# Second batch's kept parts on GpSimd's queue, other PSUM banks for scores and first values, other buffers for its keys, early fetches one by one

## What is computed

```python
x = L0_attn_x                                  # (2, 2048, 2048) float32, two batches
xn = (x - mean(x)) / sqrt(var(x) + 1e-5)       # over the last axis
q, k, v = split(xn @ Wqkv + bqkv, 3)           # 512 features each
attn = softmax(q @ k.T / sqrt(512)) @ v        # within a batch
gate = one_hot_softmax(top_k((xn @ Wq_w.T) @ keys.T, 16))   # 64 experts
z = (xn @ A_w.T) * gate                        # 64 experts x rank 8 = 512 features
out = x + attn @ Wo + bo + (z @ B_w.T) * 2.0
```

## Time and profile before

| | |
|---|---|
| median of 3 runs | 2750.1 us |
| the profiled execution | 2748.78 us, span 2746.8 us |
| granted clock of TensorE, mean over the span | 0.992 |
| TensorE | 97% busy, 11728 matmuls |
| VectorE, ScalarE, GpSimd | 68%, 36%, 18% busy |
| DMA | 648.29 MB, 236 GB/s on the mean |

### The profile page before, as it was taken

How to read it: one execution, slowest core, us unless ns; L and a number is a source line. 1 busy time by engine, 2 the same in 40 slices (tenths; PEclk the granted TensorE clock), 3 DMA queues, 4 the chain that set the end, 5 groups by cost and what they waited for, 6 DMA issues and landing times.

```text
span 2746.8 us, 32502 instructions
## 1 busy us (share of the span) xinstructions
PE 2655.9 (97%) x11728; PEld 2173.1 (79%) x11728; DVE 1856.9 (68%) x2311; ACT 976.5 (36%) x1289; POOL 494.5 (18%) x414
## 2 busy tenths in 40 slices
PE   6997999999999999999999999999998999999998
PEld 4776878878878888887887888887886888888787
DVE  6965876467755677676847476485773846658687
ACT  3562325622365224433334432224332233322311
POOL 1010000000000001111103332324213241232540
PEclk9999999999999999999999999999999999999999
DMA  8699666454564557766787758668676685866876
GB/s 308 203 342 290 230 207 200 147 167 153 170 207 148 175 182 239 236 211 237 265 301 254 265 193 291 230 241 322 232 273 261 220 312 196 292 229 231 299 260 221
DMA packets 256770, 648.29 MB, mean 236 GB/s; under 512 B 26720, under 2 KB 51424, under 8 KB 252384
## 3 DMA queue, kind: packets, MB, share of 16 engines
q1 hardware_dynamic: 205136, 487.80, 51.3%
q0 software_dynamic: 25616, 94.38, 9.5%
q10 hardware_dynamic: 25856, 63.99, 6.7%
HBM read 499.27 MB, written 146.83 MB: 235 GB/s over the span
## 4 chain that ended last, share of the span: by engine, by line
PE 84%; DMA 6%; DVE 5%; issue 2%; ACT 2%; SPq 0%; ACTq 0%; DVEq 0%
PE psum L803 36%; PE psum L1922 15%; PE psum L1924 15%; PE psum L1923 15%; DMA w_raw<-t_scratch 2%; PE psum L738 2%; DMA r_lo<-split_scratch 1%; DMA stat_scratch<-mv 1%; DVE w_lo L864 1%; ACT w_hi L524 1%; DMA w_raw<-W_blocks 1%; ACT rows L594 1%; PE psum L2008 0%; DVE s_lo L869 0%; DVE xb L951 0%
## 5 line engine op out<-in xcount | busy, mean ns | idle before, releaser
L864 DVE TENSOR_TENSOR w_lo<-w_raw,w_hi 128x1024 fp32r<-128x1024 f32 x224 | 274.0, 1223 | 386.4 <-ACT w_hi L524 386.3
L524 ACT ACTIVATE w_hi<-w_raw 128x1024 fp32r<-128x1024 f32 x224 | 237.5, 1060 | 735.0 <-PE psum L803 611.4
L803 PE MATMUL psum<-w_hi,s_hi 128*128 128x512 f32 x896 | 351.8, 393 | 22.4 <-DVE w_lo L864 21.3
L803 PE MATMUL psum<-s_hi,w_hi 128*128 128x512 f32 x896 | 352.3, 393 | 11.2 <-DVE s_lo L869 6.7
L803 PE MATMUL psum<-s_lo,w_hi 128*128 128x512 f32 x896 | 350.5, 391 | 0.0
L803 PE MATMUL psum<-w_lo,s_hi 128*128 128x512 f32 x896 | 350.3, 391 | 0.0
L803 PE MATMUL psum<-s_hi,w_lo 128*128 128x512 f32 x896 | 350.2, 391 | 0.0
L803 PE MATMUL psum<-w_hi,s_lo 128*128 128x512 f32 x896 | 350.2, 391 | 0.0
L803 PEld LDWEIGHTS psum<-w_hi,s_hi 128*128 128x128 f32 x896 | 169.1, 189 | 64.0 <-DVE w_lo L864 23.6
L2117 POOL TENSOR_TENSOR run_sum<-run_sum,prob 128x512 f32<-128x512 f32 x98 | 158.9, 1622 | 318.7 <-ACT prob L1761 311.7
L1922 PE MATMUL psum<-q_hi,r_hi 128*128 128x512 f32 x512 | 200.4, 391 | 11.9 <-issue 10.5
(11 more groups left out here) (197 smaller groups left out, 4945.9 us busy)
## 6 DMA issues: line engine op xcount, KB each, us to landing
r_hi<-split_scratch SPq DMA_DIRECT2D x208, 512.0 KB, 3.4
r_lo<-split_scratch SPq DMA_DIRECT2D x208, 512.0 KB, 4.5
w_raw<-t_scratch SPq DMA_DIRECT2D x128, 512.0 KB, 4.3
w_raw<-W_blocks SPq DMA_DIRECT2D x96, 512.0 KB, 3.9
split_scratch<-rows POOLq DMA_DIRECT2D x56, 512.0 KB, 4.2
part_out<-x POOLq DMA_DIRECT2D x28, 1024.0 KB, 12.5
out<-part_out SPq DMA_DIRECT2D x28, 1024.0 KB, 8.1
rows<-x ACTq DMA_DIRECT2D x26, 1024.0 KB, 5.1
```

Source lines behind the costliest of these rows:

```text
L524: nc.scalar.activation(w_hi[:, s % RAW], w_raw[:, s % RAW], ACT.Copy).then_inc(s_whi, 1)
L803: mm = pe.matmul(psum[:, bank, :], stationary, moving, start=(k == 0 and n == 0 and not chained), stop=(k == HK - 1 and n == 2), skip_grou ...
L864: nc.vector.tensor_tensor(w_lo[:, s % RAW], w_raw[:, s % RAW], w_hi[:, s % RAW].bitcast(F32), ALU.subtract).then_inc(s_wlo, 1)
```

## The change

- **Stores**: for t = 4, GpSimd issues the stores of kept parts (`keep` in its program), between the loads of x in S4 and between the sums in V4; they count on semaphores of their own (`b_late`). SyncE keeps only the first batch's. GpSimd's `scores(4)` loads two quarters of x (C22, C12), stores S4's items 0 to 3, loads C21 and C11, stores items 4 to 7, and then adds the bias.
- **Key buffers**: the raw tiles of S4 lie in eight places: items 0 to 3 in the quarters C11 and C21 of `part`, items 4 to 7 in `q_raw` and `p1_part`.
- **Banks**: scores of tiles 0 to 6 use banks 5, 2, 3, 4, 6, 0, 1. V0 uses banks 3, 4, 5, 6 and V1 banks 0, 1, 7, 6; the others stay with `BANK_B`.
- **V0**: the broadcast of group 1's maxima comes behind item 2 in place of item 1, and ScalarE takes it one item later.
- **Early fetches**: `ahead.sync` is called five times, at (5, 1), (5, 3), (5, 5), (5, 7) and (6, 1): first the queries, then one key item each.

```diff
@@ -133,6 +133,7 @@
 CHAINED = (1, 4, 6)
 SPLIT_TILES = 32
+AHEAD_AT = [(5, 1), (5, 3), (5, 5), (5, 7), (6, 1)]
@@ -490,8 +491,8 @@
                             store_kq(g, C22, b)
                             store_kq(g, C12, b)
-                    if not more and (idx, s) == (5, 1):
-                        ahead.sync(sp)
+                    if not more and (idx, s) in AHEAD_AT:
+                        ahead.sync(sp, AHEAD_AT.index((idx, s)))
                     if not more and idx == NI - 1 and s > PART:
@@ -1370,8 +1371,8 @@
         return (BANK_A, BANK_B)[(q + (w == NQ - 1)) % 2]
-    V_BANK = BANK_B
-    S_BANK = [(2 + k) % 7 for k in range(KEYT)]
+    V_BANKS = {0: [3, 4, 5, 6], 1: [0, 1, 7, 6]}
+    S_BANK = [(5, 2, 3, 4, 6, 0, 1)[k % 7] for k in range(KEYT)]
     S_LAST = [max(k for k in range(KEYT) if S_BANK[k] == b) if b < 7 else None for b in range(8)]
@@ -1401,8 +1402,14 @@
         return sum(1 if is_split(m) else 2 for m in range(n % RING, n + 1, RING))
-    def kept(n):
-        return sum(is_split(m) for m in range(n % RING, n, RING))
+    def slot_kept(engine, n):
+
+        before = [m for m in range(n % RING, n, RING) if is_split(m)]
+        late = [m for m in before if ITEMS[m][1] == BATCH]
+        if late:
+            engine.wait_ge(b_late[n % RING], 32 * len(late))
+        elif before:
+            engine.wait_ge(b_keep[n % RING], 32 * len(before))
@@ -1497,7 +1505,8 @@
         kind, t, i = ITEMS[n]
         if kind == "S" and t == BATCH:
-            return (q_raw, p1_part)[i % RING // 2][:, i % 2 * 2:i % 2 * 2 + 2, :]
+            tiles = (part[:, C11 * QT:(C11 + 1) * QT, :], part[:, C21 * QT:(C21 + 1) * QT, :], q_raw, p1_part)[i // 2]
+            return tiles[:, i % 2 * 2:i % 2 * 2 + 2, :]
         if t == 0:
@@ -1523,6 +1532,9 @@
         return attn[:, (w // 2 * 2 + row - 1) % 3, rows, :] if col == 1 else zT[:, row - 1, rows, :]
+    def bias_order(w):
+        return (C22, C12, C21, C11) if w == BATCH - 2 else (C22, C21, C12, C11)
+
     def out_quarter(w, c):
@@ -1548,6 +1560,9 @@
         return 2 * DT * ((t + 1) // 2)
+
+    def v_bank(t):
+        return V_BANKS.get(t, BANK_B)
@@ -1578,7 +1593,7 @@
         def keep_before(n):
-            while KEPT["next"] < len(SPLITS) and SPLITS[KEPT["next"]] < n:
+            while KEPT["next"] < 2 * LEN["S"] and SPLITS[KEPT["next"]] < n:
                 keep(SPLITS[KEPT["next"]])
@@ -1598,11 +1613,12 @@
                 if n >= RING and not is_split(n - RING):
                     sp.wait_ge(b_used, n - RING + 1)
-                if i < RING and t == BATCH and kind == "S":
-                    if i < 2:
-                        sp.wait_ge(b_qlo, 2 * (t + 1))
+                if t == BATCH and kind == "S":
+                    if i < 4:
+                        sp.wait_ge(b_st[(C11, C21)[i // 2]], 16 * 2)
                     else:
-                        sp.wait_ge(b_zt, z_done(t - 1))
+                        sp.wait_ge(b_lo, order - RING + 1)
+                        sp.wait_ge(b_qlo, 2 * (t + 1)) if i < 6 else sp.wait_ge(b_zt, z_done(t - 1))
                 elif i < RING and t == BATCH:
@@ -1683,19 +1699,18 @@
                     sp.dma_start(b_out[:], bo.rearrange("(a d) -> a d", a=1).to_broadcast([P, C])
                                  ).then_inc(b_z, 16)
-            if t == BATCH:
-                keep_before(number("S", t + 1, 0))
...
             return
         if early == "fetch":
-            first.early_stored(sp)
-            first.queries_free(sp)
-            queries(0)
-            first.raw_free(sp)
-            for i in range(RING):
-                fetch("S", 0, i)
+            if step == 0:
+                first.early_stored(sp)
+                first.queries_free(sp)
+                queries(0)
+                first.raw_free(sp)
+            else:
+                fetch("S", 0, step - 1)
             return
@@ -1716,7 +1731,7 @@
             act.wait_ge(b_raw[slot], 16 * landed(n))
             wait(act, b_used, n - RING + 1)
-            wait(act, b_keep[slot], 32 * kept(n))
+            slot_kept(act, n)
             nc.scalar.activation(r_pair(r_hi, n), raw_tile(n), ACT.Copy).then_inc(b_hi, 1)
@@ -1887,7 +1902,7 @@
                     exponential(1, 8 + 2 * i)
                     exponential(1, 9 + 2 * i)
-                if t == 0 and i == 2:
+                if t == 0 and i == 3:
                     take_maximum(1)
@@ -1939,8 +1954,8 @@
             elif t == 1:
                 pe.wait_ge(b_copy, S_LAST[bank] + 1)
-            elif bank in V_BANK:
-                pe.wait_ge(b_mul, inverted(t - 1) + V_BANK.index(bank) + 1)
+            elif bank in v_bank(t - 1):
+                pe.wait_ge(b_mul, inverted(t - 1) + v_bank(t - 1).index(bank) + 1)
             else:
@@ -1998,7 +2013,7 @@
             if m < 3:
                 if t == 1:
-                    pe.wait_ge(b_copy, 2 * KEYT)
+                    pe.wait_ge(b_mul, inverted(0) + DT)
                 else:
@@ -2063,14 +2078,16 @@
         def value_bank_free(t, d):
-            bank = V_BANK[d]
+            bank = v_bank(t)[d]
             if t == 0:
+                pe.wait_ge(b_copy, KEYT + S_LAST[bank] + 1)
+            elif t == 1:
                 if bank == MISC_S:
                     pe.wait_ge(b_mall, 1)
+                elif bank in v_bank(0):
+                    pe.wait_ge(b_mul, inverted(0) + v_bank(0).index(bank) + 1)
                 else:
                     pe.wait_ge(b_copy, KEYT + S_LAST[bank] + 1)
-            elif t == 1:
-                pe.wait_ge(b_mul, inverted(0) + d + 1)
             else:
@@ -2093,7 +2110,7 @@
                 if t == 0 and i == 0:
                     transpose_maxima(1, MISC_V)
-                if t == 0 and i == 1:
+                if t == 0 and i == 2:
                     broadcast_maxima(1, MISC_V)
@@ -2116,6 +2133,13 @@
                     nc.gpsimd.tensor_tensor(run_sum[:], run_sum[:], prob_tile(t, k), ALU.add).then_inc(b_acc, 1)
+        def keep(kind, t, i):
+            n = number(kind, t, i)
+            slot = n % RING
+            pool.wait_ge(b_lo, SPLITS.index(n) + 1)
+            for half, r in enumerate((r_hi, r_lo)):
+                pool.dma_start(split_scr[home(n), half], r[:, slot, :].bitcast(F32)).then_inc(b_late[slot], 16)
+
         def load_rows(w, c):
@@ -2126,6 +2150,8 @@
                 pool.wait_ge(b_plo, 2 * KEYT)
                 pool.wait_ge(b_acc, 2 * MAX_STEPS)
+            if w == BATCH - 2 and c in (C11, C21):
+                pool.wait_ge(b_lo, SPLITS.index(number("S", BATCH, {C11: 1, C21: 3}[c])) + 1)
             if w == BATCH - 1 and c in (C11, C21):
@@ -2147,9 +2173,14 @@
                 sums(0, range(1, 8))
             elif t >= 2:
-                for c in OUT_ORDER:
-                    load_rows(t - 2, c)
-                for c in OUT_ORDER:
+                order = bias_order(t - 2)
+                for half in (order[:2], order[2:]):
+                    for c in half:
+                        load_rows(t - 2, c)
+                    for i in range(LEN["S"] // 2):
+                        if t == BATCH:
+                            keep("S", t, i + (0 if half == order[:2] else LEN["S"] // 2))
+                for c in order:
                     add_bias(t - 2, c)
@@ -2170,7 +2201,11 @@
                 sums(1, range(8, KEYT))
             else:
-                sums(t, range(10, KEYT))
+                for i in range(LEN["V"]):
+                    if t == BATCH:
+                        keep("V", t, i)
+                    if i < 6:
+                        sums(t, range(10 + i, 11 + i))
             if t == NQ - 1:
@@ -2304,13 +2339,13 @@
                 if q == 0:
                     for c in (C22, C21, C12):
-                        dve.wait_ge(b_xb, 4 * QT * w + (OUT_ORDER.index(c) + 1) * QT)
+                        dve.wait_ge(b_xb, 4 * QT * w + (bias_order(w).index(c) + 1) * QT)
                         add_product(w, c, j, bank_set(w, q)[j])
...
                     add_product(w, C22, j, bank_set(w, q)[j])
                 elif q == 2:
-                    dve.wait_ge(b_xb, 4 * QT * w + (OUT_ORDER.index(C11) + 1) * QT)
+                    dve.wait_ge(b_xb, 4 * QT * w + (bias_order(w).index(C11) + 1) * QT)
                     add_product(w, C11, j, bank_set(w, q)[j])
```

More of the change, by code:

```diff
@@ L1451, in phase_b @@
     b_keep = [sem(f"b_keep{i}") for i in range(RING)]
+    b_late = [sem(f"b_late{i}") for i in range(RING)]
     b_hi = sem("b_hi")
@@ L1618, in fetch @@
             sp.wait_ge(b_used, n - RING + 1)
-            sp.wait_ge(b_keep[slot], 32 * kept(n))
+            slot_kept(sp, n)
             for half, r in enumerate((r_hi, r_lo)):
@@ L2031, in product_bank_free @@
                 elif w == NQ - 2:
-                    pe.wait_ge(b_mul, inverted(NQ - 1) + V_BANK.index(bank) + 1)
+                    pe.wait_ge(b_mul, inverted(NQ - 1) + v_bank(NQ - 1).index(bank) + 1)
                 else:
@@ L2086, in values @@
```

(6 more changed lines are left out.)

## The result

| | before | after |
|---|---|---|
| median of 7 runs each, us | 2752.51 (2748.93 to 2756.19) | 2744.73 (2743.05 to 2746.82) |
| ratio after / before | | 0.9971, 95% interval 0.9960 to 0.9982 |
| profiled execution, us | 2748.8 | 2743.4 |
| its span, us | 2746.8 | 2741.3 |

The change makes the kernel 7.8 us faster by the medians and 5.4 by the two profiled executions. The forecast was 14.7 faster (2735.4); the measured 2744.7 lies above the range given. So some 9 us of the gain are missing in the profiled pair, and that is what this part is about.

What follows compares the result with a forecast made beforehand. TensorE, busy 97% of the span, was taken as the bound; only its 91 us not busy and its half-clock losses could move. Seven terms summed to -14.7 us, taking the 2750.1 us median to 2735.4; range 2728.5 to 2742.5.

Steps and rivals of the forecast that it cites:

- Term 1: S5's start: moving the second batch's stores from SyncE to GpSimd removes the fetch wait and its clock loss, -12.1 us.
- rival B: S5's hole is only halved because the DMA engines are full in it; 2742 us, chance 0.10.
- rival C: S4 and V4: GpSimd's store queue becomes the bound, net +7, 2757 us, chance 0.05.
- rival D: S5 still waits in full since GpSimd's sums delay a V4 store; -2.6, 2747.5 us, chance 0.06.
- term 2: First phase: early fetches in portions remove the wait behind a weight load and its clock loss, -4.2 us.
- term 4: S0's start: first score bank 5 must wait for VectorE's part additions, +2.15 us; 3.6 with a clock loss.
- Term 5: Starts of S2 and S6: bank 5 waits for ScalarE to empty the transposed gates, +1.0 us each.
- Term 6: V3's last item and S4's start: waits for a low part and the reciprocal shrink, -1.8 us.
- Term 3: V0 and V1: later maxima broadcast and new V1 banks save time, less 1.5 of ScalarE/VectorE lead; -6.5 us.
- Term 7: O2: GpSimd's bias additions slip from S4 and slow VectorE, so TensorE waits for the diagonal; +5.8 us, bounds 0 and 7.

Runs made afterwards that it cites:

- experiment 5: Changed kernel with the query load and four early key fetches issued in a row again at (5, 1); 2747.89 us, one execution.
- experiment 4: Changed kernel with scores starting in bank 2 and bank 5 second, V0 and product banks reordered to suit; 2739.77 us, 0.9962 of before.
- experiment 2: Changed kernel with GpSimd waiting for the end of each bias addition before the next, in all eight groups; 2739.77 us, 0.9965 of before.
- experiment 6: Changed kernel with S4's bias additions for two chunks behind its first two stores, the others behind its last two; 2731.23 us, 0.9932 of before.
- experiment 10: Changed kernel with S4's sixteen bias additions starting behind VectorE's maximum over key tile 11, 2.6 us later planned; 2739.35 us, one execution.
- Experiment 8: Changed kernel with the broadcast of group 1's maxima behind item 1 of V0 again and ScalarE's copy one item earlier; 2745.06 us, one execution.
- experiment 3: Kernel before with one more wait: GpSimd's S4 bias additions held until S4's last key item is split; 2756.57 us, 1.0025 of before.
- experiment 9: Changed kernel with S4's sixteen bias additions starting 1.9 us later, once ScalarE has copied key tile 11; 2741.05 us, one execution.
- experiment 7: Changed kernel with both S4's bias additions split and moved early and scores starting in bank 2; 2725.56 us, 0.9912 of before.
- experiment 1: Changed kernel with S4's sixteen bias additions cut into four groups of four, one behind each of its last four stores; 2742.45 us, 0.9972 of before.

## Why the prediction was wrong

**The terms that held.** Term 1, -12.1: measured -10.6 in V4 and -1.5 in S5, together -12.1. The moved stores' issues took 0.53 to 0.57 us each and landed in 4.3 to 12.3 us (median 7.5). V4 took 44.42 us, as long as V2, which has no stores, and S5 starts without idle time, so rivals B, C and D fall. The Trainium skill's box on "DVE blocks DMA" (SBUF — State Buffer) did not bite: no issue of a store took longer than that. (Whether any VectorE operation beside them was in a two-port mode, which the box is about, no trace here shows.) Terms 2 and 4, -4.2 and +2.15, sum to -2.05: measured -2.3 at S0's first matmul. That this agrees to 0.3 is partly luck, given the scatter of the first phase; what shows the terms is local: the first-phase hole is gone, and 2.25 us are lost at S0; experiment 5 brings 4.3 back, experiment 4 takes S0's wait away. The 3.6 us that term 4 named for the case of a clock loss came too, in experiments 2, 6 and 10, where the clock fell behind the same wait. Term 5, +1.0 each: 0.88 at S2 and 0.99 at S6. Term 6, -1.8: -1.9. One reading of the prediction is off, and enters no term: TensorE's idle time ahead of the first phase's first matmul in before is 27 us (33.0 less 5.8 busy), not about 22.

**Term 3, -6.5**: -4.7 up to S2's first matmul, -5.7 without the 1.0 that term 5 has already. The removed broadcast wait did give its 6 us (V0 went from 55.5 to 49.5). The 1.9 us for V1's first banks did not come: TensorE still stands 2.23 us ahead of V1 and loses the clock behind it (4.1 us in all, as before). Experiment 8 shows that part of the broadcast's 6 us was to be had only once: with that wait put back, the hole ahead of V1 shrinks by 2 us. The bank is no longer what it waits for; the low part is (1503.35 + 0.6, TensorE at 1504.07), and that has a reciprocal of 3.34 us ahead of it:

```profile
1500.09 3.34 DVE L2283 RECIPROCAL inv_sum<-psum 128x512 f32<-128x512 f32 x1
1503.35 1.22 DVE L2265 TENSOR_TENSOR p_lo<-part_out,p_hi 128x512 fp32r<-128x512 f32 x2
```

What was late next was what the prediction had charged with 1.5 us, the lead of the chain of ScalarE and VectorE, and it took the gain of the banks.

**Term 7, +5.8 forecast, +12.2 measured: this is the step that failed.** Its place and its cause were right: the additions stood behind S4's eighth keep and ran from 31.7 us into S4 (forecast: 1932, that is 32.6) in place of earlier, and TensorE waited for VectorE. The size was not. The term priced VectorE beside GpSimd by the rows in which the two take turns, a two-input operation of 1.22 us in 2.3. Where turns were taken the price held or nearly so: 6.1 in experiment 2 and 7.0 in experiment 3. Experiments 9 and 10, with a later end of the additions, had 8.3 and 9.7, above the bound of 7 that the term gave itself: the diagonal's four small operations, which I left at 0.87, took 2.16 to 4.22. In after turns were not taken, and one maximum stood behind fifteen additions. TensorE stopped not at the diagonal, two items into O2, but at O2's first matmul.

The prediction drew on the Trainium skill (SBUF — State Buffer, "Who interferes with whom"), and the page has more than I drew from it: its section "SBUF: two separate sides" calls the shared port pair an exclusive lock, held by whoever starts first for the whole instruction, while the other fully blocks. For the turns the trace agrees: a maximum waits at most for the one addition that is running (0.69 becomes up to 1.78). For the shut-out the rule alone doesn't give the price. If the waiting operation always went next, it would wait for at most one addition, 1.28 us; 18.46 was measured, so in after it did not go next. The runs decide.

**What was not in the sum.** O3 grew by 1.7 us. The loads of x for group 3 now stand behind the last keep:

```profile
2060.94 0.53 POOL L2141 DMA_DIRECT2D split_scratch<-r_lo  x1
2061.47 3.00 POOL L2158 DMA_DIRECT2D part_out<-x  x4
2089.51 26.10 POOL L2167 TENSOR_TENSOR part_out<-part_out,b_out 128x512 f32<-128x512 f32 x16 [25.04 <-DMA part_out<-x]
```

In before the first was issued at 2044.77 and the other three from 2056.98 on, and the additions began at 2079.19. Here the four loads take 25 us to land, the DMA engines being full (share 1.02, 393 GB/s from 2061 to 2089.5). The additions end at 2115.6, 3.8 us inside O3, and TensorE waits 0.85 us for the diagonal at 2124.22 (1.0 lost by the starts). Another 0.45 us are lost at 2170.59, behind one of VectorE's additions of a product; that one was not followed up. The prediction spoke of these loads only as one burden less on S5's fetch, and did not follow them to their own readers: term 7's question, asked for one of two groups. V7 and O6, +0.9, were not traced to a cause.

Summed on the profiled pair: term 7 +6.4, O3 +1.7, term 3 +0.8, V7 and O6 +0.9, against the forecast's -14.7: -4.9, and -4.9 was measured. That the sum closes so well includes the first phase's -2.3, which could have been some us more or less.

**What stays open.** What decides whether GpSimd's additions let VectorE in. It isn't the offset alone: in experiment 2 the maximum also came 1.9 us into the run and had its turn, but there every addition waited for the one before. It isn't the moment within the running addition either. In after a maximum of S2 came 0.64 us into an addition and took 1.20 us, and the one of 18.46 us came 0.64 us into its addition too:

```profile
1571.41 1.30 POOL L2167 TENSOR_TENSOR part_out<-part_out,b_out 128x512 f32<-128x512 f32 x1
1572.05 1.20 DVE L2244 TENSOR_TENSOR run_max<-run_max,prob 128x512 f32<-128x512 f32 x1 [1.75 <-ACT prob L1766]
```
```profile
1923.52 1.28 POOL L2167 TENSOR_TENSOR part_out<-part_out,b_out 128x512 f32<-128x512 f32 x1
```

Long operations without harm stand in after's S6 (7.49 us, 13.0 us into its run) and in experiments 6 (6.59) and 7 (5.64). These and the 18.46 us ones end 0.5 to 1.1 us behind the run's last addition; in experiment 1 one got in ahead of the end of its run. There is none in the eight runs of additions of before, and none in those of experiments 3, 9 and 10, which have no waits between the additions. So the eight clean runs of experiment 2 are one execution that fits the remedy, and do not prove it; experiments 9 and 10 show that another start can avoid the shut-out, not which start does.

## What to carry to other kernels

If a run of GpSimd operations on SBUF moves, ask what VectorE does in its new place, and price two cases: taking turns (here 6 to 10 us of TensorE's time, for a chain that it waits for) and standing behind the whole run (18.5 us for one operation, 12 us of TensorE's time). Such a run belongs where VectorE has slack of its own full length: splitting it so that it ended before the chain began was worth all 12 us, putting waits between its additions came with only half. When an instruction is queued behind a new one on its engine, follow each of the instructions behind it, loads too, to its reader in every group, not only in the first.

## What the runs showed of the hardware that was not expected

- A VectorE operation with two SBUF inputs that takes 0.69 us alone took 18.46 us beside back-to-back GpSimd additions (1.24 us each, never interrupted); the same length, to 0.01 us, came at the same offset in three further kernels. Others took 7.49, 6.59, 6.25, 5.64 and 4.35 us. With a wait between the additions the longest was under 2.5, but so it was in before and in experiments 3, 9 and 10, which have none.
- VectorE operations of 128x128 elements lose about as much each as large ones: of the four that build the diagonal each took 0.28 us alone, and three of the four took 1.30 beside GpSimd's additions (experiments 9 and 10; the four together 0.87 and 4.22).
- The length of a hole alone did not tell whether the clock fell. The wait ahead of S0 left TensorE idle for 2.1 us in after and in seven experiments; behind it the clock fell in three of them (experiments 2, 6 and 10: granted clock 0.50, 1.6 to 1.7 us lost) and stayed at its upper level in the other five kernels. Ahead of V1 TensorE was idle for 2.23 us in after, with 1.7 us lost at the lower level behind it, and for 2.23 and 2.26 us in experiments 4 and 7, where the clock stayed up. In before it fell behind 2.33 us at this place, in experiment 3 it did not behind 2.34. Sizes of single executions, those of term 3 and experiment 4 among them, carry this uncertainty of 1.5 us.
